# Depth rounds that keep their masks, earlier counts and edge rows, and dot products moved into the first attention step

## What is computed

```python
edge_index = jnp.stack([src, dst])
h = jnp.maximum(_layernorm(x, axis=-1), 0.0)
x = x + _L0_gnn_ref(h, edge_index, ...)        # two graph convolutions, 64 -> 128 -> 64
h = jnp.maximum(_layernorm(x, axis=-1), 0.0)
x = x + _L1_gnn_ref(h, edge_index, edge_attr_64, ...)   # relu(x[src] + edge_attr), summed by dst, linear
h = jnp.maximum(_layernorm(x, axis=-1), 0.0)
x = x + _L2_gnn_ref(h, L2_gnn_attn_w, L2_gnn_temp, src, dst)
h = jnp.maximum(_layernorm(x, axis=-1), 0.0)
x = x + _L3_gnn_ref(h, src, dst)               # ten steps of a normed segment sum

# _L2_gnn_ref, the attention layer, K = 8
for k in range(K):
    s1 = h @ w_src
    s2 = h @ w_dst
    e = jax.nn.leaky_relu(s1[src] + s2[dst])
    a = _edge_softmax(e, dst, n)
    h = jax.ops.segment_sum(h[src] * a[:, None], dst, num_segments=n)
    th = th + h * temp[k + 1]
```

## Time and profile before

| | us |
|---|---|
| median of 3 runs (9848.82 to 9856.18) | 9849.85 |
| the profiled execution | 9845.43 |
| its span | 9843.8 |
| POOL busy | 6361.7 (65%) |
| VectorE busy | 5536.8 (56%) |
| TensorE busy | 1625.2 (17%) |
| ScalarE busy | 593.6 (6%) |
| DMA, mean over the span | 58 GB/s |

### The profile page before, as it was taken

How to read it: one execution, slowest core, us unless ns; L and a number is a source line. 1 busy time by engine, 2 the same in 40 slices (tenths; PEclk the granted TensorE clock), 3 DMA queues, 4 the chain that set the end, 5 groups by cost and what they waited for, 6 DMA issues and landing times.

```text
span 9843.8 us, 60633 instructions
## 1 busy us (share of the span) xinstructions
PE 1625.2 (17%) x7434; PEld 1157.5 (12%) x7434; DVE 5536.8 (56%) x16716; ACT 593.6 (6%) x1219; POOL 6361.7 (65%) x6415
## 2 busy tenths in 40 slices
PE   5634231210244302540012200000000000000000
PEld 1223131110233201430011100000000000000000
DVE  6769484683999861436678845545446443333310
ACT  0011010000111100110000000000001000000000
POOL 6767755527477777767767577666640677777777
PEclk9855555555555555555555555555555555555555
DMA  0022120100234432333333322242221121333320
GB/s 10 11 80 95 49 78 31 52 28 0 71 114 124 115 88 67 91 84 90 91 93 100 86 45 50 43 42 39 37 27 45 43 47 40 44 42 39 35 26 19
DMA packets 588778, 568.96 MB, mean 58 GB/s; under 512 B 420588, under 2 KB 426657, under 8 KB 588624
## 3 DMA queue, kind: packets, MB, share of 16 engines
q0 software_dynamic: 193184, 160.50, 12.3%
q10 hardware_dynamic: 368192, 328.20, 10.0%
q1 hardware_dynamic: 27346, 79.76, 2.4%
HBM read 214.35 MB, written 357.51 MB: 58 GB/s over the span
## 4 chain that ended last, share of the span: by engine, by line
POOL 44%; issue 24%; DVE 19%; DMA 11%; POOLq 1%; DVEq 1%; PE 0%; SPq 0%; ACTq 0%; ACT 0%
POOL G L446 23%; POOL look L446 5%; DVE G L1740 5%; POOL X L446 4%; POOL pair L446 4%; POOL seatmap L450 4%; POOL out L450 3%; DMA G<-in_edge_attr,idxs 1%; DVE st L1253 1%; DMA G<-tab_d,idxs 1%; DMA alt_d<-G 1%; DMA G<-alt_d,idxs 1%; DMA tab_e<-rowsE 1%; DVE xm L1278 1%; DVE G L1989 1%
## 5 line engine op out<-in xcount | busy, mean ns | idle before, releaser
L446 POOL DMA_INDIRECT G<-tab_e,idxs x644 | 681.7, 1058 | 230.3 <-issue 188.8
L446 POOL DMA_INDIRECT G<-tab_d,idxs x616 | 640.2, 1039 | 221.2 <-issue 176.6
L446 POOL DMA_INDIRECT look<-flagtab,idxs x588 | 614.9, 1046 | 206.8 <-issue 170.2
L2118 DVE TENSOR_TENSOR G<-G,chn 128x896 f32<-128x896 f32 x76 | 83.2, 1095 | 938.8 <-DMA G<-tab_e,idxs 548.0
L446 POOL DMA_INDIRECT X<-in_x,dst_gat x392 | 421.1, 1074 | 249.1 <-issue 125.8
L446 POOL DMA_INDIRECT G<-alt_e,idxs x420 | 444.7, 1059 | 154.7 <-issue 127.6
L446 POOL DMA_INDIRECT G<-tab_c,idxs x392 | 441.9, 1127 | 142.9 <-issue 117.7
L974 PE MATMUL TR<-w4T,shared 128*128 128x64 f32 x2356 | 488.7, 402 | 190.2 <-ACT shared L753 190.2
L446 POOL DMA_INDIRECT G<-tab_b,idxs x392 | 419.2, 1069 | 141.1 <-issue 113.5
L446 POOL DMA_INDIRECT pair<-lookup,idxs x392 | 418.5, 1068 | 140.3 <-issue 116.5
L974 PEld LDWEIGHTS TR<-w4T,shared 128*128 128x128 f32 x2356 | 475.4, 312 | 283.5 <-issue 283.5
(11 more groups left out here) (465 smaller groups left out, 7530.5 us busy)
## 6 DMA issues: line engine op xcount, KB each, us to landing
raw<-G ACTq DMA_DIRECT2D x84, 448.0 KB, 3.6
tab_d<-rowsD ACTq DMA_DIRECT2D x56, 469.0 KB, 2.6
tab_d<-G ACTq DMA_DIRECT2D x56, 469.0 KB, 2.8
xin<-in_x SPq DMA_DIRECT2D x56, 448.0 KB, 5.6
tab_a<-rowsA ACTq DMA_DIRECT2D x56, 448.0 KB, 2.5
tab_b<-rowsB ACTq DMA_DIRECT2D x56, 448.0 KB, 2.8
out<-shared ACTq DMA_DIRECT2D x56, 448.0 KB, 5.6
tab_c<-rowsC ACTq DMA_DIRECT2D x56, 448.0 KB, 2.6
```

The lines of the kernel that those rows point to most:

```text
L446: pool.indirect_dma_start(to, None, table, bass.IndirectOffsetOnAxis(ap=index, axis=0), bounds_check=bound, oob_is_err=False).then_inc(s, 16)
L2118: v.tensor_tensor(g, g, wide(chn[:, 1, :]), ALU.mult).then_inc(dve_step, 1)
```

## The change

1. `squeeze` keeps its nine masks (`moved1` for the first round, `moved_n` for the others) and shifts the payload in place. `stretch` only applies them in reverse: one backward, in-place predicated copy a step, nothing else.
2. VectorE raises `flags_ready` after `segment_flags` and a new `counts_ready` after `ranks`, both ahead of `squeeze`; POOL stores the flags first, then the counts. For the fifth look-up both are raised together.
3. POOL gathers 5 of the 28 chunks of edge attributes (`HEAD`) before the gather of x, released by `seats_ordered` after the second sort.
4. Dense tiles no longer compute dot products, edge rows only the second one. The first attention step is written out on its own (`first=True`): it computes both on the gathered rows, sets column D+2 to one, and has no reciprocal and no test of the width.

```diff
@@ POOL, depth rounds
             with pool.Fori(0, LEVELS + 1):
                 pool.wait_ge(flags_ready, r_fl.more(1))
                 pool.sem_inc(pool_waited, 1)
+                pool.dma_start(flagtab.rearrange("(p j) f -> p (j f)", p=P), flags[:, :]).then_inc(flags_stored, 16)
+                pool.wait_ge(counts_ready, r_cr.more(1))
+                pool.sem_inc(pool_waited, 1)
                 pool.dma_start(counts, cn[:, 0:1]).then_inc(counts_stored, 16)
-                pool.dma_start(flagtab.rearrange("(p j) f -> p (j f)", p=P), flags[:, :]).then_inc(flags_stored, 16)
@@ POOL, after attr_rows is defined (the gather of x stood ahead of it)
+            pool.wait_ge(seats_ordered, 1)
             attr_rows(0, True)
-            with pool.Fori(1, NCH) as c:
+            with pool.Fori(1, HEAD) as c:
+                attr_rows(c, False)
+
+            pool.wait_ge(order_ready, 1)
+            last_row(x)
+            for j in range(COLS):
+                gather(X[:, j, :], x, dst_gat[:, j:j + 1], x_gathered)
...
+            with pool.Fori(HEAD, NCH) as c:
                 attr_rows(c, False)
@@ VectorE, dense tiles and edge rows
-                dots(to, R)
+                dots(to, R, (1,))
...
-            def dense_dots(s):
-                dots(row_d[s][:, :, :], CH)
+            def dense_d_ready(s):
                 dve.sem_inc(rows_ready, 1)
@@ VectorE, squeeze and stretch
-                    v.tensor_single_scalar(bit, d, s, op=ALU.bitwise_and).then_inc(dve_step, 1)
-                    dve.wait_ge(dve_step, nth())
-                    v.scalar_tensor_tensor(e, bit, 0.0, d, ALU.is_equal, ALU.mult)
-                    v.tensor_copy(q, p).then_inc(dve_step, 1)
-                    dve.wait_ge(dve_step, nth())
-                    v.copy_predicated(e[:, 0:COLS - s], bit[:, s:COLS], d[:, s:COLS])
-                    v.copy_predicated(q[:, 0:COLS - s], bit[:, s:COLS], p[:, s:COLS]).then_inc(dve_step, 1)
-                    dve.wait_ge(dve_step, nth())
...
+                    v.tensor_single_scalar(moved[n], d, s, op=ALU.bitwise_and).then_inc(dve_step, 1)
+                    dve.wait_ge(dve_step, nth())
+                    v.scalar_tensor_tensor(e, moved[n], 0.0, d, ALU.is_equal, ALU.mult)
+                    v.copy_predicated(pays[0][:, 0:COLS - s], moved[n][:, s:COLS], pays[0][:, s:COLS]).then_inc(dve_step, 1)
+                    dve.wait_ge(dve_step, nth())
+                    v.copy_predicated(e[:, 0:COLS - s], moved[n][:, s:COLS], d[:, s:COLS]).then_inc(dve_step, 1)
+                    dve.wait_ge(dve_step, nth())
+
+            def stretch(frm, moved):
+
+                v.tensor_copy(pays[0], frm).then_inc(dve_step, 1)
+                dve.wait_ge(dve_step, nth())
+                for n in range(8, -1, -1):
+                    s = 1 << n
+                    v.copy_predicated(pays[0][:, s:COLS][:, ::-1], moved[n][:, s:COLS][:, ::-1],
+                                      pays[0][:, 0:COLS - s][:, ::-1]).then_inc(dve_step, 1)
                     dve.wait_ge(dve_step, nth())
@@ VectorE, the rounds
                 segment_flags()
+                dve.sem_inc(flags_ready, 1)
                 ranks()
-                squeeze(qs)
+                dve.sem_inc(counts_ready, 1)
+                moved = moved1 if n == 0 else moved_n
+                squeeze(qs, moved)
@@ VectorE, after the second sort
             in_order(bit, steps_of[0])
+            dve.sem_inc(seats_ordered, 1)
@@ VectorE, step_d, now step_d(k, first=False)
+                    if first:
+                        dots(g, CH)
+                        v.memset(g[:, :, D + 2:D + 3], 1.0)
+                        v.tensor_copy(s1, g[:, :, D]).then_inc(dve_step, 1)
+                        dve.wait_ge(dve_step, nth())
...
-            with dve.Fori(1, K2 + 1) as k:
+            fresh()
+            step_d(1, True)
+            begin()
+            with dve.Fori(2, K2 + 1) as k:
```

More of the change, by code:

```diff
@@ L194, in _build @@
         bit = early(30).bitcast(i32)
-        list1, dist1, listI = early(31), early(32).bitcast(i32), early(33).bitcast(i32)
+        list1, listI = early(31), early(33).bitcast(i32)
+        moved1 = [early(41 + n).bitcast(i32) for n in range(9)]
+        moved_n = [early(50 + n).bitcast(i32) for n in range(9)]
         key, code, keys = early(34).bitcast(i32), early(35), [early(36), early(37)]
@@ L332, in _build @@
         EARLY = COLS - CH * K3
+        HEAD = 5
         LEAD, LEVELS = 1, 4
@@ L542, in _ @@
                 pool.sem_inc(look_done, 1)
-            pool.wait_ge(order_ready, 1)
-            last_row(x)
-            for j in range(COLS):
-                gather(X[:, j, :], x, dst_gat[:, j:j + 1], x_gathered)
-                if j % (2 * CH) == 2 * CH - 1:
-                    pool.wait_ge(x_gathered, 16 * (j + 1))
-            gather(X[:, FC, :], x, fidx[:, F_DST:F_DST + 1], x_gathered)
             r_ag = [Reached(pool, f"pool_ag{h}") for h in (0, 1)]
@@ L1273, in xcols, with dots @@
                 return X[:, ds(c * CH, CH), :]
-            def dots(to, R):
-                for k in (0, 1):
+            def dots(to, R, which=(0, 1)):
+                for k in which:
                     v.tensor_tensor(xm[:, 0:R, :], to[:, :, 0:D], flat_rows(attn[:, k * D:(k + 1) * D], R),
@@ L1488, in _ @@
                 dve.wait_ge(look_done, r_ld.more(1))
-                stretch(got, dist1 if n == 0 else hi0)
-                v.tensor_tensor(live, live, pays[1], ALU.mult).then_inc(dve_step, 1)
+                stretch(got, moved)
+                v.tensor_tensor(live, live, pays[0], ALU.mult).then_inc(dve_step, 1)
                 dve.wait_ge(dve_step, nth())
@@ L1940, in _, with step_d @@
             dve.sem_inc(step_done, 1)
-            def step_d(k):
+            def step_d(k, first=False):
                 v.tensor_copy(wcol[:, :], WB[:, ds(k, 1)])
@@ L1953, in step_d @@
+                if first:
+                    with dve.Fori(0, NCH // 2) as i:
                         fresh()
                         for s in (0, 1):
-                            c = 2 * i + s
-                            g = G[:, s, :, :]
-                            r1, s1, e0, e1, a, p, rd, rw = (sm[:, n, :] for n in range(8))
-                            v.tensor_copy(chn[:, 0, :], cols(cont, c))
-                            v.tensor_copy(chn[:, 1, :], cols(s2E, c))
-                            v.tensor_copy(chn[:, 2, :], cols(pen, c)).then_inc(dve_step, 1)
@@ L1984, in step_d @@
-                            dve.wait_ge(dve_step, nth())
-                            dve.wait_ge(exp_ready, r_exp.more(1))
-                            v.tensor_tensor(a, expd[:, 0:CH], chn[:, 0, :], ALU.mult)
-                            v.tensor_tensor(p, expd[:, CH:2 * CH], r1, ALU.mult).then_inc(dve_step, 1)
-                            dve.wait_ge(dve_step, nth())
-                            v.tensor_tensor(g, g, wide(p, AW), ALU.mult).then_inc(dve_step, 1)
-                            dve.wait_ge(dve_step, nth())
@@ L1991, in step_d @@
-                            chain(s, AW, a)
-                            v.reciprocal(rd, g[:, :, D + 2]).then_inc(dve_step, 1)
-                            dve.wait_ge(dve_step, nth())
-                            v.tensor_tensor(cols(s2V, c), g[:, :, D + 1], rd, ALU.mult)
-                            v.tensor_scalar(rw, rd, wk[:, 0:1], None, ALU.mult).then_inc(dve_step, 1)
-                            dve.wait_ge(dve_step, nth())
-                            v.tensor_tensor(agg[:, :, :], g[:, :, 0:D], wide(rw), ALU.mult).then_inc(dve_step, 1)
@@ L1998, in step_d @@
-                            dve.wait_ge(dve_step, nth())
-                            dve.sem_inc(used[s], 1)
-                            v.tensor_tensor(xcols(c), xcols(c), agg[:, :, :], ALU.add).then_inc(dve_step, 1)
-                            dve.wait_ge(dve_step, nth())
+                            attention_chunk(2 * i + s, s)
+                else:
+                    wide_to = dve.value_load(WI[0:1, ds(k, 1)], min_val=0, max_val=COLS)
+                    with dve.Fori(0, NCH // 2) as i:
+                        with dve.If(i * (2 * CH) < wide_to):
+                            fresh()
+                            for s in (0, 1):
+                                attention_chunk(2 * i + s, s)
```

116 lines of the change are left out of this document (67 added, 49 removed).

## The result

The changed kernel takes 9579.3 us (median of 4 runs, 9574.4 to 9582.5), the kernel before 9849.3 beside it: ratio 0.9727, 95% interval 0.9714 to 0.9740, faster by 270 us. The forecast was 9582 us with a range of 9552 to 9641. The profiled execution has a span of 9580.5 us, 263.3 less than that of before. Beside the runs e5 to e8 the kernel before took 10285 us and not some 9850, so the times of these four are not compared with the others.

The account below looks back on a forecast made before the run. The prediction saw a queue of gathers on POOL, with gains where POOL idles or VectorE paces it. Terms summed to -267.9 us on 9845.4, giving 9577.5; the median stands 4.4 higher: 9582 us, range 9552 to 9641.

Parts of the forecast that it names:

- Squeeze and stretch: Sort rounds on VectorE: four shorter squeezes -9.4 us, one list copy less a round -1.2, four shorter stretches -62.4.
- Counts: Look-up rounds: four of five VectorE waits for counts, 11.2 us each, hidden behind the squeeze, -44.6 us.
- Rival (c): Look-up rounds: counts not hidden because their store waits behind 200 KB of flags; +44.6, 9627 us; chance 0.07.
- The +2 for the flags going first: Fifth look-up: flags stored ahead of the counts cost +2 us, the size of one issue and its traffic.
- Dense pair under the fourth look-up: VectorE under the fourth look-up: a half pair without products gains 3.65 us after waiting 1.0 for TensorE; -7.3 us.
- Edge rows early: Fifth look-up to the sweep over `tab_a`: five edge chunks fill POOL's idle time before x; -101 us.
- Sweep over `tab_c`: VectorE loses products and reductions: -63.6 us if VectorE paces to the end, -45 if POOL does; -58 taken.
- Rival (b): Sweep over `tab_c`: POOL becomes the bound, -45 us instead of -58; 9595 us; chance 0.10.
- First attention step: Products added there: last chunk's bare work +4.3 us, gathers held by VectorE +10; sum +14, bounds +4.3 and +41.
- Rival (a): First attention step: the second product catches its gather in each chunk, +27 us, 9609 us; chance 0.12.
- Rival (f): First attention step: new products hold no gather, +4.3 us instead of +14; 9572 us; chance 0.04.
- The pattern of the prediction: POOL gathers starting 0.05 to 0.95 us after a wide two-input VectorE instruction end 0.88 us after it; reductions hold nothing.

Follow-up runs that it names:

- e5: Changed kernel with each first-attention-step product with attn replaced by a reduction (four reductions a chunk); first step 598.9 us, total time not compared.
- e8: Changed kernel with the loop over chunk pairs of attention steps 2 to 8 split into pairs 0 to 4 and 5 to 13; total time not compared.
- e2: Changed kernel with squeeze and stretch as before, masks computed twice; 9654.8 us, ratio 0.9802, +75.5 on the changed kernel.
- e1: Changed kernel with counts_ready raised behind the squeeze again; 9626.8 us, ratio 0.9773, +47.5 on the changed kernel.
- e3: Changed kernel with all 28 chunks of edge rows after the gather of x again; 9651.2 us, ratio 0.9803, +71.9 on the changed kernel.
- e4: Changed kernel with dot products back in dense tiles and edge rows, one loop over all eight attention steps; 9660.7 us, ratio 0.9812, +81.4.
- e10: Changed kernel with reductions in place of the first attention step's products (four reductions a chunk); 9571.0 us, ratio 0.9717, first step 591.3 us.
- e11: Changed kernel with 20 chunks of edge rows ahead of the gather of x, not 5; 9669.7 us, ratio 0.9811, +90.
- e9: Changed kernel with the loop over chunk pairs of attention steps 2 to 8 split in two behind one width test; 9540.5 us, ratio 0.9683.

## Why the prediction was right, point by point

- **Squeeze and stretch** (-9.4, -1.2, -62.4): right. A step lost 0.24 us (forecast 0.26), a stretch takes 5.38 us (5.4), the backward price is the forward one, and e2 gives 75.5 for 73 (71.7 in the stretches that it changes).
- **Counts** (-44.6): right, e1 gives 47.5 (42.6 in the stretches that it changes). Cover and chain were as worked out. Rival (c) is out. The +2 for the flags going first at the fifth look-up does not show: 11.3 us of wait there, as before.
- **Dense pair under the fourth look-up** (-7.3): -7.5. The rows that the prediction names give a wait of 2765.97 - 2765.11 = 0.86 us for TensorE, not the 1.0 that it took; the changed kernel shows 0.93 (the row at 2779.92 in the last section).
- **Edge rows early** (-101): -106.0 measured. x began where it should. e3 and e4 split it: some 78 for the order, 15 for the shorter stretch (as long as x comes first), and 12 to 16 for the dense pairs without products. The last part was in the sum only as fewer chunks beside dense pairs; that the gathers beside the remaining dense pairs would be held less (9.6 us) was not.
- **Sweep over `tab_c`** (-58): -63.8, under the lower of its two bounds, and the step that bounded it failed. POOL, not VectorE, paces now: the wait of POOL for stored sums, 19 times in the earlier trace rows, is gone from the trace. I had given that case -45. But a chunk went from 22.20 to 20.38 us between POOL's index copies ((5578.11 - 4978.70) / 27 and (5292.15 - 4742.01) / 27), 49.3 us over 27 chunks, of which the waits are 29.1 at the most. The other 20 are gathers that are no longer held: what the gathers of over 1.10 us took beyond 1.00 fell from 47.4 to 22.9 us. The bound of -45 had left out this term, though the prediction's next sentence named it at half of 0.7 us a chunk. e4 gives the 64.0 back. Rival (b), -45, is out, though POOL did become the bound. The kernel before, then the changed one:

```profile
5578.11 0.19 POOL L589 COPY idxs<-idxA 128x14 int32 x1 [1.78 <-DMA raw<-G]
...
4742.01 0.19 POOL L601 COPY idxs<-idxA 128x14 int32 x1 [2.11 <-DMA tab_c<-rowsC,fidx]
...
5292.15 0.53 POOL L601 COPY idxs<-idxA 128x14 int32 x1
...
5328.05 1.00 POOL L451 DMA_INDIRECT tcar<-raw,fidx  x1 [15.55 <-DMA raw<-G]
...
5357.47 1.03 POOL L455 DMA_INDIRECT tab_d<-rowsD,fidx  x1 [27.11 <-DVEq L1374]
```

- **First attention step** (+14): +18.4. The bare part behind the last chunk's gathers is 4.1 (forecast 4.3). The held gathers came to 12.3 us more, against 10: the second product, which the prediction let pass by a margin of 0.02 us, caught its gather in 9 chunks of 28. Rival (a) was right in a third of the chunks; a phase that moves by 0.1 us from chunk to chunk does not stay on one side of an edge 0.05 us wide. e3, with the same instructions in this step, has +10.3, so that the term came within 5 us is in part luck. Rival (f), no hold at all, is out (e10).
- **Attention steps 2 to 8** (0): +16.7. Not in the sum. The prediction took it that steps whose instructions don't change don't change. VectorE's code moved, and 76 pairs passed over cost 0.20 us more each, 16 us. So the sum left out a term, and it was not small.
- **Not in the sum either**: -4.2 at the `pair` gathers and -2.0 over `tab_a` and `tab_b`. The `pair` gathers end between 1226.4 and 1239.9 us in the kernels here (e5 to e8 left out), and two things move them. Held gathers and scatters (over 1.10 us, beyond 1.00) add up to 35.2 us before and 36.1 in e4, whose dense tiles compute products, and to 27.3 to 30.5 in the others: enough for the -4.2. And POOL's waits for the `pair` gathers to land add up to 20.4 to 23.3 us in most kernels, but to 31.9, 33.6 and 32.7 in e1, e2 and e11, which end 11 to 12 us later; no edit of theirs bears on that, and its cause is open.

The total, -263.3 in the spans for -267.9 forecast, is better than its parts, and that is luck: the rows of the table that came out better than forecast are 20 us better together, the others 24 us worse. (In the medians it is -270, within what two medians vary.) The range's width was needed for the parts.

## What to carry to other kernels

Where one engine issues everything, a gain is read off its idle times, and each part then adds to the others, as long as no two of them fill the same idle time (the fifth stretch and the early edge rows did). A bound for "the other engine paces" must be made with that engine's speed after the change, not before: the edit that relieves one engine may also stop disturbing the other. A loop that passes over unused turns has a price per turn; if what follows is on the path, test a whole block of turns with one branch.

## What the runs showed of the hardware

- The price of passing over a loop's body of some 90 instructions hung on where the code lay: 0.54 to 0.74 us a turn in kernels with the same loop, and both in one program (e9). The Trainium skill, "Advanced Engine Details and Errata", section "Control Flow Timing", gives a compare-and-branch some 108 ns; a turn passed over has two of them in the order of instructions, and the readings are 2.5 to 3.4 times that sum. In these traces the next instruction starts 0.09 us after a compare-and-branch that falls through (the end of the loop), near that figure, and 0.17 to 0.32 us after one that jumps.
- A TENSOR_TENSOR or SCALAR_TENSOR_TENSOR of 128x896 with both inputs in SBUF holds a POOL gather or scatter that starts 0.06 to 0.95 us after it, until 0.84 to 0.96 us (mostly 0.88) behind its own end; one that starts 0.03 us after it passes, and at 0.05 both were seen. In the changed kernel 562 started 0.06 to 0.90 us after such an instruction, and all were held. Four TENSOR_REDUCE of the same length in a row held none (e10).
- Where the inputs lie counts, not the name or the length of the instruction. The sum below reads `TR`, which the kernel allots in PSUM and TensorE writes: in the changed kernel 77 gathers and scatters started 0.06 to 0.95 us after one of these, and none took over 1.01 us. And one input is enough for this TENSOR_SCALAR of f32 in SBUF: all 14 gathers that started under the one of `tab_c`'s sweep (10 before, 4 after) took 1.35 to 1.36 us, again to 0.87 us behind its end. The pattern of the prediction, "two inputs", was too narrow there. Changed kernel, VectorE and POOL, twice:

```profile
2779.92 1.09 DVE L1360 TENSOR_TENSOR agg<-TR,b1b 128x896 f32<-128x896 f32 x1 [0.93 <-PE TR L996]
...
2780.17 1.00 POOL L451 DMA_INDIRECT X<-in_x,dst_gat  x1 [0.30 <-issue]
...
5030.46 0.63 DVE L1874 TENSOR_SCALAR G<-G 128x896 f32<-128x896 f32 x1
...
5030.61 1.35 POOL L451 DMA_INDIRECT G<-tab_c,idxs  x1 [0.30 <-issue]
```

- COPY_PREDICATED, backward and in place, costs as much as forward: 0.578 us against 0.58 for 391 columns of f32.
